# Attention aggregation of a two-layer graph network: one transfer a step, a resident table of destinations, and one of two products moved from GpSimd to VectorE

## The reference

```
alpha = ex / (den[dst] + 1e-16)
...
hs = (m2_s @ Ws_vlin).reshape(e, H, AS_)
hv = jnp.einsum('ecx,cd->edx', m2_v, Wv_vlin).reshape(e, H, AV, 3)
h = jnp.concatenate([hs, hv.reshape(e, H, AV * 3)], axis=-1)
agg = jax.ops.segment_sum(alpha * h, dst, num_segments=n)
```

## Time and profile before

| | us |
|---|---|
| median of 3 runs | 8251.5 (8251.28 to 8253.19) |
| span of the profiled execution | 8256.1 |
| aggregation, first matrix on VectorE to last matmul | about 840 |
| VectorE busy over the whole span | 7559.8 (92%) |
| TensorE busy over the whole span | 7100.0 (86%) |
| GpSimd busy over the whole span | 5566.3 (67%) |
| ScalarE busy over the whole span | 5166.1 (63%) |

### The profile page before, as it was taken

One profiled execution on the slowest core, in us unless ns is written; L12 is line 12 of the kernel. 1 busy time (PEld: TensorE's weight loads), 2 busy tenths in 40 slices (PEclk: granted clock), 3 DMA queues, 4 the chain that ended last, 5 costly groups with the idle time before them and its releaser, 6 DMA issues. The chain is left out here.

```text
span 8256.1 us, 202673 instructions
## 1 busy us (share of the span) xinstructions
PE 7100.0 (86%) x48227; PEld 5913.7 (72%) x48227; DVE 7559.8 (92%) x18614; ACT 5166.1 (63%) x17382; POOL 5566.3 (67%) x5953
## 2 busy tenths in 40 slices
PE   6999999999999999999999477779888888888888
PEld 4888888888888888888888366666555555555556
DVE  5999999999999999999999655554999999999999
ACT  2666666666666666666666311113777777777776
POOL 2777777777777777777776177771777777777773
PEclk5999999999999999999999699995999999999999
DMA  3443344334343444433343166651333333333332
GB/s 104 107 108 105 105 106 106 106 106 105 105 105 105 105 106 105 105 105 105 105 105 96 61 177 177 177 157 38 94 91 89 89 89 89 88 89 89 89 89 60
DMA packets 854751, 855.52 MB, mean 104 GB/s; under 512 B 478992, under 2 KB 636560, under 8 KB 854160
## 3 DMA queue, kind: packets, MB, share of 16 engines
q0 software_dynamic: 241920, 413.20, 20.5%
q1 hardware_dynamic: 612176, 437.39, 18.7%
q10 hardware_dynamic: 576, 4.01, 0.1%
HBM read 705.56 MB, written 148.44 MB: 103 GB/s over the span
## 5 line engine op out<-in xcount | busy, mean ns | idle before, releaser
L1219 POOL DMA_INDIRECT agg<-tab_conv,ce_idx x1808 | 1708.8, 945 | 866.0 <-issue 621.5
L464 POOL DMA_INDIRECT ae_gsrc<-tab_src,ae_idx x1616 | 1534.1, 949 | 751.8 <-issue 447.0
L467 POOL DMA_INDIRECT ae_gdst<-tab_dst,ae_idx x1616 | 1645.9, 1019 | 540.0 <-issue 538.2
L1308 PE MATMUL psum<-ce_prod,ce_plain 128*128 128x384 f32 x3616 | 1539.6, 507 | 328.3 <-DVE ce_prod L1281 275.5
L1293 ACT ACTIVATE ce_prod<-ce_raw,ce_y 128x64 f32<-128x64 f32 x5424 | 1464.0, 332 | 0.0
L1291 ACT ACTIVATE ce_prod<-ce_raw,ce_y 128x160 f32<-128x160 f32 x1808 | 752.6, 416 | 515.2 <-DVE ce_raw L1240 515.2
L709 ACT ACTIVATE ae_second_t<-psum 128x512 f32<-128x512 f32 x1212 | 731.7, 604 | 504.7 <-PE psum L619 499.0
L1310 PEld LDWEIGHTS psum<-ce_prod,ce_plain 128*128 128x128 f32 x3616 | 687.6, 190 | 479.4 <-issue 1.2
L1308 PEld LDWEIGHTS psum<-ce_prod,ce_plain 128*128 128x128 f32 x3616 | 547.0, 191 | 475.3 <-DVE ce_plain L1269 340.8
L627 PE MATMUL psum<-pack_sb,ae_first_t 128*128 128x200 f32 x3232 | 851.8, 345 | 2.2 <-ACT ae_first_t L705 2.0
L985 PE MATMUL psum<-ag_exval,ag_hot 128*128 128x164 f32 x3616 | 614.9, 314 | 237.2 <-issue 129.6
(11 more groups left out here) (215 smaller groups left out, 19257.6 us busy)
## 6 DMA issues: line engine op xcount, KB each, us to landing
ag_val<-h_dram SPq DMA_DIRECT2D x452, 320.0 KB, 3.2
h_dram<-ae_hout SPq DMA_DIRECT2D x404, 320.0 KB
agg<-in_query SPq DMA_DIRECT2D x452, 128.0 KB
ae_rin<-in_rin SPq DMA_DIRECT2D x404, 128.0 KB
agg<-tab_conv,ce_idx POOLq DMA_INDIRECT x1808
ae_gsrc<-tab_src,ae_idx POOLq DMA_INDIRECT x1616
ae_gdst<-tab_dst,ae_idx POOLq DMA_INDIRECT x1616
ag_idx<-in_eidx SPq DMA_DIRECT2D x452, 4.0 KB, 2.7
```

Of the source, the lines that this page charges most:

```text
L464: pool.indirect_dma_start(gsrc[t.slot4][:, k, :], None, g["tab_src"], bass.IndirectOffsetOnAxis(ap=idx[t.slot4][:, k:k + 1], axis=0))\
L467: pool.indirect_dma_start(gdst[t.slot4][:, k, :], None, g["tab_dst"], bass.IndirectOffsetOnAxis(ap=idx[t.slot4][:, 4 + k:5 + k], axis=0))\
L1219: pool.indirect_dma_start(node[t.slot8][:, k, :], None, g["tab_conv"], bass.IndirectOffsetOnAxis(ap=idx[t.slot8][:, k:k + 1], axis=0))\
L1308: pe.matmul(b_a[t.slot], plain[t.slot4][:, k, :], prod[t.slot][:, k, 96:480], start=(k == 0), stop=False, skip_group_check=True)
```

## The change

`idx` and its transfer go. A new input `dst_of` holds the destinations of all edges by edge group (128 x 1616 int32), and SyncE loads it once in the softmax stage, behind three loads of its own. SyncE reads the tile numbers of eight steps at once, at every eighth step. ScalarE copies the step's four destination columns out of `dst_of` (`ends`, with a conversion to float) and the step's shares into PSUM (`shares`, two places), ahead of its two old copies. VectorE makes `hot` from `ends`, now after a wait for ScalarE, and multiplies the scalar columns by `shares`. GpSimd keeps the vector columns and reads no number. The semaphore `weighted` becomes `scalars_done` and `vectors_done`; ScalarE has a new wait for the scalar product of two steps before.

```
+LOADS = -(-STEPS // 8) * 8
...
+                g["dst_of"] = upper.enter_context(nc.sbuf_tensor("dst_of", [P, 4 * SUPER], I32))
+                g["dst_in"] = upper.enter_context(nc.semaphore("dst_in"))
...
-                dve.tensor_copy(g["step_s"][:, :], s_f[:, :])
+                dve.tensor_copy(g["step_s"][:, 0:STEPS], s_f[:, :])
+                dve.memset(g["step_s"][:, STEPS:LOADS], 0)
...
                 for i in range(3):
                     sp.dma_start(dst[i][:, :], io["dst3"][i]).then_inc(loaded, 16)
+                sp.dma_start(g["dst_of"][:, :], io["dst_of"]).then_inc(g["dst_in"], 16)
...
+def eight(nc, kind, table, at, most):
+
+    _, values = nc.values_load_multi_w_load_instructions(table[0:1, bass.ds(at.n, 8)], engines=[kind], min_val=0, max_val=most)
+    return values
...
+        shares = [banks[5 + u][:, 0:4 * H].rearrange("p (k h) -> p k h", k=4) for u in range(2)]
...
                 def body(t):
-
-                    step_loads(sp, t, g["step_s"], ((weighted, t.n - 7), (hot_done, t.n - 7)),
-                               ((idx[t.slot8][:, :], io["eidx"], loaded[t.slot8]),
-                                (val[t.slot8][:, :, :].rearrange("p k c -> p (k c)"), g["h_dram"], loaded[t.slot8])))
+                    if t.slot8 == 0:
+                        s[:] = eight(nc, ENG.SP, g["step_s"], t, SUPER - 1)
+                    wait(sp, scalars_done, t.n - 7)
+                    wait(sp, vectors_done, t.n - 7)
+                    sp.dma_start(val[t.slot8][:, :, :].rearrange("p k c -> p (k c)"),
+                                 g["h_dram"][bass.ds(s[t.slot8], 1)].rearrange("a p c -> (a p) c")).then_inc(loaded[t.slot8], 16)
...
                 def body(t):
-                    s = pool.value_load(g["step_s"][0:1, bass.ds(t.n, 1)], min_val=0, max_val=SUPER - 1)
-                    ex = g["alpha"][:, bass.ds(4 * s, 4), :]
-                    pool.wait_ge(loaded[t.slot8], 32 * (t.eighth + 1))
+                    pool.wait_ge(loaded[t.slot8], 16 * (t.eighth + 1))
                     wait(pool, summed, t.n - 3)
-                    pool.tensor_tensor(exval[t.slot4][:, :, 0:CS].rearrange("p k (h c) -> p k h c", h=H),
-                                       val[t.slot8][:, :, 0:CS].rearrange("p k (h c) -> p k h c", h=H),
-                                       ex.unsqueeze(3).to_broadcast([P, 4, H, AS]), ALU.mult)
                     pool.wait_ge(ex_done, t.n + 1)
...
             def _(act):
+                act.wait_ge(g["dst_in"], 16)
+
...
-                    wait(act, weighted, t.n - 3)
+                    wait(act, vectors_done, t.n - 3)
+                    wait(act, scalars_done, t.n - 1)
                     wait(act, summed, t.n - 3)
+                    act.activation(ends[t.slot4][:, :], dst_of[:, bass.ds(4 * s, 4)], ACT.Copy)
+                    act.activation(shares[t.slot], ex, ACT.Copy)
...
-                        dve.wait_ge(loaded[t.slot8], 32 * (t.eighth + 1))
                         wait(dve, summed, t.n - 3)
+                        dve.wait_ge(ex_done, t.n + 1)
                         dve.scalar_tensor_tensor(hot[t.slot4][:, :, :], iota.unsqueeze(1).to_broadcast([P, 4, P]),
                                                  g["block128"][:, bass.ds(t.n, 1)],
-                                                 idx[t.slot8][:, 4:8].unsqueeze(2).to_broadcast([P, 4, P]),
+                                                 ends[t.slot4][:, :].unsqueeze(2).to_broadcast([P, 4, P]),
                                                  ALU.add, ALU.is_equal).then_inc(hot_done, 1)
+                        dve.wait_ge(loaded[t.slot8], 16 * (t.eighth + 1))
+                        dve.tensor_tensor(exval[t.slot4][:, :, 0:CS].rearrange("p k (h c) -> p k h c", h=H),
+                                          val[t.slot8][:, :, 0:CS].rearrange("p k (h c) -> p k h c", h=H),
+                                          shares[t.slot].unsqueeze(3).to_broadcast([P, 4, H, AS]), ALU.mult).then_inc(scalars_done, 1)
...
                     pe.wait_ge(hot_done, t.n + 1)
-                    pe.wait_ge(weighted, t.n + 1)
+                    pe.wait_ge(scalars_done, t.n + 1)
+                    pe.wait_ge(vectors_done, t.n + 1)
```

More of the change, by code:

```diff
@@ L110, in gnn @@
         block128 = top.enter_context(nc.sbuf_tensor("block128", [P, STEPS], F32))
-        step_s = top.enter_context(nc.sbuf_tensor("step_s", [P, STEPS], I32))
+        step_s = top.enter_context(nc.sbuf_tensor("step_s", [P, LOADS], I32))
         step_b = top.enter_context(nc.sbuf_tensor("step_b", [P, STEPS], I32))
@@ L890, in step_loads @@
         sp.dma_start(out, src[bass.ds(s, 1)].rearrange("a p c -> (a p) c")).then_inc(sem, 16)
+def eight(nc, kind, table, at, most):
+    _, values = nc.values_load_multi_w_load_instructions(table[0:1, bass.ds(at.n, 8)], engines=[kind], min_val=0, max_val=most)
+    return values
 def attention_aggregate(nc, g):
-    w, banks, io, agg = g["w"], g["banks"], g["io"], g["agg"]
+    w, banks, io, agg, dst_of = g["w"], g["banks"], g["io"], g["agg"], g["dst_of"]
     W = C + H
+    ENG = mybir.EngineType
     with ExitStack() as ctx:
@@ L903, in sem @@
             return ctx.enter_context(nc.semaphore(f"ag_{name}"))
-        idx = [sb(f"idx{u}", [P, 8], I32) for u in range(8)]
         val = [sb(f"val{u}", [P, 4, C]) for u in range(8)]
@@ L908, in attention_aggregate @@
         hot = [sb(f"hot{u}", [P, 4, P]) for u in range(4)]
+        ends = [sb(f"ends{u}", [P, 4]) for u in range(4)]
         loaded = [sem(f"loaded{u}") for u in range(8)]
-        zeroed, hot_done, weighted, ex_done, summed, added = (sem(x) for x in (
-            "zeroed", "hot_done", "weighted", "ex_done", "summed", "added"))
+        zeroed, hot_done, scalars_done, vectors_done, ex_done, summed, added = (sem(x) for x in (
+            "zeroed", "hot_done", "scalars_done", "vectors_done", "ex_done", "summed", "added"))
         iota = banks[4][:, 0:P]
+        shares = [banks[5 + u][:, 0:4 * H].rearrange("p (k h) -> p k h", k=4) for u in range(2)]
         with nc.Block() as block:
@@ L916, in _ @@
             def _(sp):
+                s = []
                 def body(t):
-                    step_loads(sp, t, g["step_s"], ((weighted, t.n - 7), (hot_done, t.n - 7)),
-                               ((idx[t.slot8][:, :], io["eidx"], loaded[t.slot8]),
-                                (val[t.slot8][:, :, :].rearrange("p k c -> p (k c)"), g["h_dram"], loaded[t.slot8])))
+                    if t.slot8 == 0:
[4 more added lines that the diff above has]
+                                 g["h_dram"][bass.ds(s[t.slot8], 1)].rearrange("a p c -> (a p) c")).then_inc(loaded[t.slot8], 16)
                 loop(sp, body, 0, STEPS, STEPS)
@@ L937, in body @@
                                        wide[t.slot4][:, :, :].unsqueeze(3).to_broadcast([P, 4, 3 * H, AV]), ALU.mult)\
-                        .then_inc(weighted, 1)
+                        .then_inc(vectors_done, 1)
                 loop(pool, body, 0, STEPS, STEPS)
@@ L1522, in lay_inputs @@
         rin=np.concatenate([left, right], 2), yall=y.reshape(4 * SUPER, P, 4).transpose(1, 0, 2),
-        query=query)
+        query=query, dst_of=dst.reshape(4 * SUPER, P).T)
 def kernel(**inputs):
```

## The result

The kernel after takes **7993.1 us** (median of 4 runs, 7987.1 to 7997.8), against 8252.35 for the kernel before on the same chip (8251.3 to 8258.3): a ratio of 0.9683, interval 0.9669 to 0.9696, 259 us less. The forecast was 8010.

What follows compares the result with a forecast made beforehand. SyncE's own instructions bound the aggregation at 1.856 us a step, VectorE's queue afterwards at 1.32. (1.856 - 1.32) x 451 = 242 us gained, 1 lost: 8251.5 - 241 = 8010 us, range 7945 to 8145.

Steps and rivals of the forecast that it cites:

- SyncE bound before: Aggregation before the change: SyncE's own instructions, not waits for engines, set the step at 1.83 to 1.86 us.
- GpSimd next in line, at 1.39: Aggregation before the change: GpSimd's two products need 0.58 + 0.81 = 1.39 us a step, the next bound after SyncE.
- SyncE afterwards: SyncE with one transfer and eight reads at once: 0.85 us a step, between 0.68 and 1.31, under the bound.
- VectorE bounds, by its queue: Aggregation after the change: VectorE's queue sets 1.11 + 0.17 + 0.04 = 1.32 us a step, engine time 1.23; chance 0.67.
- ScalarE: mis-sized, harmless: ScalarE's step with two new copies at 0.18 us each: 1.1 us, at most 1.25.
- rival 5: ScalarE's copies behind the two-place `shares` ring make the kernel slower, for example 2.0 us a step, 8319 us; chance 0.04.
- The load of `dst_of`: Loading the 827 KB table in the softmax stage delays the loads ahead of it by 1 us.
- 2, transfers bound: Aggregation's transfers stay at 226 GB/s, 1.45 us a step, up to 1.6; 8069 to 8137 us; chance 0.14.
- DMA share 0.85 or more: Expected sign in the aggregation: DMA engines busy 0.85 or more of the stage, at 248 GB/s.
- 3, the block number read only once the product has started: VectorE reads the block number only after its product starts: 1.77 us a step, 8214 us; chance 0.07.
- 4, TensorE at 1.11 to 1.22: VectorE issues more freely and TensorE bounds the aggregation step at 1.11 to 1.22 us; 7916 to 7966 us; chance 0.06.
- 6: SyncE still bounds the aggregation, eight reads costing more together than singly: near 1.85 us a step, no change; chance 0.02.

Runs made afterwards that it cites:

- e5: Kernel after with single step-number reads on SyncE and both products on GpSimd, keeping only the table and one transfer; 8039.8 us, ratio 0.9742.
- e1: Kernel before with SyncE reading eight step numbers at once, both transfers and both products on GpSimd kept; 8112.0 us, ratio 0.9829.
- e2: Kernel before with only the scalar product moved to VectorE, SyncE's two transfers and single reads kept; 8254.5 us, ratio 1.000.
- e3: Kernel after with the scalar product back on GpSimd, with GpSimd's own read of the step number; 8044.7 us, ratio 0.9747.
- e4: Kernel after with SyncE reading one step number each step, still with one transfer; 8020.1 us, ratio 0.9717.
- e6: Kernel after with a quarter of the scalar product back on GpSimd; 7986.9 us, ratio 0.9676.
- e7: Kernel after with half of the scalar product back on GpSimd; 7982.6 us, ratio 0.9672.
- e9: Kernel after with VectorE reading two block numbers at every second step; 7993.5 us, ratio 0.9680.
- e10: Kernel after with a quarter of the scalar product on GpSimd and VectorE's block numbers read in pairs; 7980.6 us, ratio 0.9661.
- e11: Kernel after with a quarter of the product on GpSimd, paired block reads and VectorE's loop unrolled 16 times; 7971.6 us, ratio 0.9654.
- e12: Kernel after with the shares in SBUF instead of PSUM; 8014.0 us, ratio 0.9704.
- e8: Kernel after with VectorE reading eight block numbers at once for eight steps; 8268.9 us, ratio 1.002.

## Why the prediction was right

**SyncE bound before: shown.** e5 takes away one issue of two and e1 seven reads of eight, and each alone shortens the step; e2 leaves SyncE alone and changes nothing. In before and in e1 SyncE's queue waits for no engine.

**GpSimd next in line, at 1.39: shown** by e3 and e5, to 0.01 us.

**SyncE afterwards: right side, mis-sized.** I took 0.85 us a step between 0.68 and 1.31. With e1's 3.1 us for eight reads it is 0.65 + 0.39 = 1.04. This 1.04 is an estimate, since in the kernel after SyncE is held by the full ring. It stays below the bound, and the burst hides behind the ring, as said. The eight reads were needed: without them (e4) SyncE bounds at 1.341, 27 us more.

**VectorE bounds, by its queue: right, both queue terms mis-sized.** The engine's 0.66 + 0.33 + 0.24 = 1.23 us measured 1.22. For the queue I had 1.11 + 0.17 + 0.04 = 1.32. As I read e6 and e7, the new wait and instruction cost 1.17 - 1.11 = 0.06 us instead of 0.17, and the turn of the loop 0.78 / 8 = 0.10 instead of 0.04. The two errors have opposite signs and cancel in part. Together 1.27 instead of 1.32, so the stage gave 265 us where 242 were forecast. That VectorE's own instructions set the pass is shown by e6, e7 and what the trace has ready ahead of each of its instructions. The split into a step and a turn is only read: five steps of eight in the kernel after are at the engine's 1.22 us and the queue shows at the turn alone, e9's lighter reads gave nothing, and e10 and e11 gave less than the split foretold. The medians show 259 of the profiles' 270.8: that of before stands 3.8 us above its median of 8252.35, that of after 7.8 below its own.

**ScalarE: mis-sized, harmless.** In order of time, its first steps:

```profile
4696.41 0.20 ACT L964 ACTIVATE ag_ends<-dst_of 128x4 f32 x1 [1.14 <-PEq L806]
4696.52 0.18 ACT L965 ACTIVATE psum<-alpha 128x16 f32 x1
4696.64 0.23 ACT L966 ACTIVATE ag_wide<-alpha 128x48 f32 x1
...
4697.23 0.20 ACT L964 ACTIVATE ag_ends<-dst_of 128x4 f32 x1 [0.26 <-issue]
```

The new copies cost 0.11 and 0.12 us each, below the lower bound of 0.14, and the step 0.82 us instead of 1.1. The integer read and the PSUM write, on which rival 5 (slower) hung, cost no more than the other copies.

**The load of `dst_of`:** 1 us forecast, none measured.

**The rivals.** 2, transfers bound near 1.45 us at 226 GB/s: no, 256 GB/s over the whole stage. The sign "DMA share 0.85 or more" didn't come, though: it is 0.77, so a step's transfer keeps the DMA engines busy for 0.77 x 1.269 = 0.98 us, less than the 1.18 us that I had from both transfers of before. A transfer takes longer from issue to landing than in before, 4.1 us instead of 3.2, but the ring absorbs it:

```profile
ag_val<-h_dram SPq DMA_DIRECT2D x452, 320.0 KB, 4.1
```

3, the block number read only once the product has started: no, the addition follows the matrix by 0.99 us, which is the engine's own time. Only in the two steps behind the loop's turn does the addition come later, by 0.12 and 0.07 us. 4, TensorE at 1.11 to 1.22: no, every addition starts at least 0.80 us after its matmuls. 5: VectorE's matrix stood idle 2.1 us in all. 6: no, though e1 shows that the eight reads cost much more than a shared load would.

## What to carry to other kernels

Find the queue that bounds from the spacing of its issues, then list what each other engine needs for a step, its queue as well: here taking away SyncE's bound was worth 0.47 us a step and stopped exactly at GpSimd's 1.39. An engine that shows no idle time can still be set by its queue; the test is to make its work shorter and see whether the loop's pass moves, and then to look whether what its instructions wait for was ready. A saving read from one engine's queue needn't hold on another's. Reading several numbers at once pays on a queue with a deep ring ahead of its users, and can cost the whole gain on one that feeds a busy engine. A group's mean can stand for no instruction of the group: look at the shortest, the median and the longest before reading it as a price.

## What was not expected of the hardware

- A load of eight numbers into registers took 0.524 us on SyncE and 1.847 us on VectorE, with 0.268 us for one on SyncE and 0.303 on VectorE. In either queue a number further costs a register operation (147 ns on SyncE, 183 on VectorE) and more, about 0.32 us in all on SyncE.
- A turn of VectorE's loop costs about 0.8 us of its queue in each pass of eight steps (an estimate from e6 and e7), which the engine's time hides in part.
- With both inputs of VectorE's product in SBUF, it and GpSimd's product beside it don't share the slowdown: one keeps its 0.41 or 0.85 us and the other takes 0.7 or 0.28 us longer. A lead of GpSimd's of about 0.02 us at the start decided which (e12).
- After 4.2 us of idle time TensorE went on at its lower level (0.50 from 5014 to 5016 us, 1.00 again from 5018 to 5022); over e8's stage the granted clock is 0.83 in the mean.
